# TensorE held back until the last table row has landed, then all four groups of four tiles in one go

## The chip, the core and the metric

The kernel runs on one core of one Trainium2 chip. The metric is the device time of one execution in microseconds (us), the median over runs. The core has a matrix engine (TensorE; PE in the rows), a vector engine (VectorE; DVE), an activation engine (ScalarE; ACT), GpSimd (POOL), which here only issues gathers, and SyncE (SP), which issues the plain transfers. Every engine works off its own list of instructions in order, and semaphores tie the lists together.

## What is computed

A batch of 2048 samples has 26 index fields and 13 dense values. Each index picks a row of 32 values from its field's table. From these rows the reference makes a linear term and a term over all products of pairs of fields, and a small network stands behind them:

```python
embed = tables[jnp.arange(FIELD_NUM)[None, :], sparse_inputs]      # 2048 x 26 x 32
p = jnp.einsum('bfe,bge->bfg', embed, embed)                       # 2048 x 26 x 26
l_z = jnp.einsum('bfe,feh->bh', embed, w_z)                        # h = 256
l_p = jnp.einsum('bfg,fgh->bh', p, w_p)
l_1 = relu(concatenate([l_z + l_p + l_b, dense_inputs], axis=-1))
h = relu(l_1 @ W1 + b1)                                            # 128
return sigmoid(h @ Wf + bf)
```

All of it is in float32.

## The kernel before

The batch is cut into 16 tiles of 128 samples, one sample per partition (`TILES`). Four tiles form a group, which the code calls a round (`ROUNDS` = 4, `TOGETHER` = 4), since one PSUM bank holds 4 x 128 columns. Each tile's 26 fields fall into two field groups (`GROUPS`): g = 0 has 16 fields in four transposes, g = 1 has 10 fields in three.

**The gather.** GpSimd issues one indirect transfer per tile and field, 16 x 26 = 416 in all (L221), tile after tile. Semaphore `landed[t][g]` counts the ones of tile t and field group g.

**The pair products.** For each tile ScalarE copies the rows of a field group into PSUM (`copy_fields`, L310, tile `ps_copy`) once they have landed; VectorE multiplies fields with fields (L252, `prod`) and adds up the products over the 32 values (L259, `pairs`). After the last rows of a tile have landed, one copy, four products and five sums are left, those of field group 1.

**The rounds on TensorE.** For each tile `turn(t)` transposes the gathered rows into PSUM `ps_turn` (L416; one bank for each field group), and the result is copied into `field_rows` (`lay`, L172 and L173). `turn_pairs(t)` transposes the pair sums into `ps_pair` (L433; three transposes), and they are copied into `pair_rows` (`lay_pairs`, L177). Once four tiles are there, `sum_lz(r)` runs 14 matmuls of 512 columns (L447) and `sum_lp(r)` six more (L458), both into `ps_h`. ScalarE makes the first hidden layer (`make_hidden0`, L333), TensorE multiplies it (`sum_h1`, L467 and L471), ScalarE makes the second (`make_hidden1`, L338), TensorE makes the logit (`sum_logit`, L476), ScalarE the sigmoid (`make_scores`, L344). The hidden layers of a round are interleaved with the transposes of the next one. A float32 matmul of 512 columns appears as two records in the trace.

**Who copies out of PSUM, and when.** `LATE` = 12. For tiles 0 to 11 ScalarE makes all the copies into `field_rows` and `pair_rows`; for tiles 12 to 15 it makes those of field group 0 and VectorE makes the rest, after all its pair products. ScalarE's list is written out by hand: between the `copy_fields` of tiles 0 to 15 stand the copies of tiles 0 to 7 and the hidden layers of round 0. So round 0's `sum_lz`, its `sum_lp` and the whole of round 1 up to its last `sum_lp` are fed while the gather runs; rounds 2 and 3 follow it. TensorE's own list has no wait of this kind: it goes on as soon as a tile has landed and the copies have freed the PSUM banks.

Of the kernel before, what the change touches and what calls it, by code (L numbers as in the profile page):

```python
# [26 lines left out]
def pnn_kernel(nc, dense, sparse, tables, w_z, w_low, w_high, l_b, W1, b1, Wf, bf, out):  # L27
# [21 lines left out]

    LATE = 12  # L50
# [25 lines left out]
    with ExitStack() as ctx:  # L76
# [69 lines left out]
        pairs_laid_act = sem("pairs_laid_act")  # L146
        pairs_laid_dve = sem("pairs_laid_dve")
# [11 lines left out]

        def laid_by_act(t):  # L160
            return NG * t if t <= LATE else NG * LATE + (t - LATE)

        def laid_by_dve(t):
            return max(0, t - LATE)

# [61 lines left out]
        def _(dve):  # L227
# [62 lines left out]
            for t in range(LATE, TILES):  # L290
                dve.wait_ge(turned, NG * t + 2)
                dve.wait_ge(lz_summed, t // TOGETHER)
                lay(nc.vector.tensor_copy, t, 1).then_inc(laid_dve, 1)
                if t > LATE:
                    dve.wait_ge(pairs_turned, t)
                    dve.wait_ge(h0_summed, (t - 1) // TOGETHER)
                    lay_pairs(nc.vector.tensor_copy, t - 1).then_inc(pairs_laid_dve, 1)
            dve.wait_ge(pairs_turned, TILES)
            lay_pairs(nc.vector.tensor_copy, TILES - 1).then_inc(pairs_laid_dve, 1)

        @block.scalar
        def _(act):
# [16 lines left out]

            def lay_pair_rows(t):  # L320
                if t >= TOGETHER:
                    act.wait_ge(h0_summed, t // TOGETHER)
                act.wait_ge(pairs_turned, t + 1)
                lay_pairs(nc.scalar.copy, t).then_inc(pairs_laid_act, 1)
# [22 lines left out]

            BOTH = range(NG)
            for t in range(TILES):
                copy_fields(t)  # L350
                if t < 4:
                    lay_rows(t, BOTH)
                    if t:
                        lay_pair_rows(t - 1)
                elif t == 7:
                    lay_pair_rows(3)
                elif t == 8:
                    make_hidden0(0)
                elif t == 9:
                    lay_rows(4, BOTH)  # L360
                    make_hidden1(0)
                elif t == 10:
                    lay_rows(5, BOTH)
                    make_scores(0)
                    lay_pair_rows(4)
                elif t == 11:
                    lay_rows(6, BOTH)
                    lay_pair_rows(5)
                elif t == 12:
                    lay_rows(7, BOTH)  # L370
                    lay_pair_rows(6)
            lay_pair_rows(7)
            for r in range(2, ROUNDS):
                make_hidden0(r - 1)
                for k in range(TOGETHER):
                    t = TOGETHER * r + k
                    lay_rows(t, BOTH if t < LATE else [0])
                    if k == 0:
                        make_hidden1(r - 1)
                    if k == 1:  # L380
                        make_scores(r - 1)
                    if k and t <= LATE:
                        lay_pair_rows(t - 1)
                if TOGETHER * (r + 1) <= LATE:
                    lay_pair_rows(TOGETHER * (r + 1) - 1)
# [5 lines left out]
        def _(pe):  # L391
# [44 lines left out]
            def sum_lz(r):  # L436
# [5 lines left out]
                if laid_by_dve(TOGETHER * (r + 1)):  # L442
                    pe.wait_ge(laid_dve, laid_by_dve(TOGETHER * (r + 1)))
# [84 lines left out]
```

## Time and profile before

| | us |
|---|---|
| median of 3 runs | 654.4 |
| lowest and highest of them | 652.64 and 654.55 |
| the profiled execution, whole | 653.79 |
| span of the profiled execution, first to last instruction | 652.0 |
| granted TensorE clock, mean share of full speed over the span | 0.688 |

Times in the rows are in us from the start of the span, durations as marked. In a row of the timeline the first number is the start and the second the duration of a merged run of instructions, "xN" their number, and the bracket the engine's idle time before it and what ended it. The clock column PEclk is the share of 2.4 GHz that TensorE was granted: 0.50 is 1.2 GHz, 1.00 is 2.4 GHz. The ends of matmuls are modelled, so their results can be ready later than the row says.

### The profile page before, as it was taken

Reading aid. Unit: us, or ns where it says so; the run is one execution under the profiler, and the core shown is the slowest. Engines: PE = TensorE matmul, PEld = TensorE weight load, DVE = VectorE, ACT = ScalarE, POOL = GpSimd, SP = SyncE. Lnnn points to the kernel's source line nnn. Section 1 sums busy time; section 2 is a strip of 40 time slices with the busy share of each in tenths; the row PEclk is TensorE's granted clock in tenths of the full one; section 3 lists DMA queues with packets and bytes.
Section 4 is the critical chain, followed back from the end, with each engine's and each line's share of the span. In section 5 each row is a group of like instructions: output and inputs, shape, how many; then the busy total and the mean of one; then the engine's idle time right before and its main releaser. Section 6 shows DMA issues by size and latency. Waiting matters only on the chain.

```text
span 652.0 us, 1736 instructions
## 1 busy us (share of the span) xinstructions
PE 136.6 (21%) x356; PEld 61.9 (9%) x356; DVE 436.1 (67%) x249; ACT 49.6 (8%) x102; POOL 417.8 (64%) x423
## 2 busy tenths in 40 slices
PE   0000000064000000310302010101800000449996
PEld 0000000031000000100001010100300000214442
DVE  3378787878787877666958767676859677650010
ACT  0000101010000000001001020101000000013201
POOL 6777777777777777677777777777777777200000
PEclk9999999997555555565556555555855555669997
DMA  6212121211121211111111112121111111000000
GB/s 138 13 14 13 13 14 13 13 13 13 13 13 13 13 12 12 12 12 12 11 12 12 12 12 12 11 13 12 11 13 11 11 12 13 5 0 1 0 1 1
DMA packets 18200, 9.06 MB, mean 14 GB/s; under 512 B 9536, under 2 KB 18189, under 8 KB 18189
## 3 DMA queue, kind: packets, MB, share of 16 engines
q0 software_dynamic: 13312, 6.84, 15.6%
q1 hardware_dynamic: 4878, 2.11, 1.3%
q14 instruction: 7, 0.06, 0.0%
q8 instruction: 3, 0.05, 0.0%
HBM read 8.91 MB, written 0.01 MB: 14 GB/s over the span
## 4 chain that ended last, share of the span: by engine, by line
POOL 58%; issue 27%; PE 8%; another core or an unknown queue 3%; ACT 2%; DMA 1%; DVE 0%; ACTq 0%
POOL rows L221 58%; PE ps_h L447 4%; PE ps_h L458 2%; PE ps_h L476 1%; PE ps_h L471 1%; ACT hidden L333 1%; PE ps_turn L416 1%; DMA rows<-in_L_rec_tables,which 1%; ACT field_rows L173 0%; PE ps_h L467 0%; PE ps_pair L433 0%; ACT scores L344 0%; DMA raw<-in_r_sparse_inputs 0%; ACT ps_copy L310 0%
## 5 line engine op out<-in xcount | busy, mean ns | idle before, releaser
L221 POOL DMA_INDIRECT rows<-in_L_rec_tables,which x416 | 417.0, 1002 | 141.0 <-issue 139.1
L252 DVE TENSOR_TENSOR prod<-ps_copy,rows 128x1536 f32<-128x1536 f32 (+6 forms) x128 | 219.4, 1745 | 138.9 <-issue 116.3
L259 DVE TENSOR_REDUCE pairs<-prod 128x96 f32<-128x3072 f32 (+2 forms) x96 | 216.6, 2270 | 0.0
L458 PE MATMUL ps_h<-pair_rows,w_pair 128*128 128x512 f32 x48 | 25.5, 688 | 209.8 <-issue 208.6
L416 PE MATMUL ps_turn<-ident,rows 128*128 128x128 f32 (+1 forms) x112 | 22.7, 351 | 221.2 <-DMA rows<-in_L_rec_tables,which 120.1
L447 PE MATMUL ps_h<-field_rows,wz 128*128 128x512 f32 (+1 forms) x112 | 55.0, 649 | 35.3 <-issue 34.2
L310 ACT COPY ps_copy<-rows 128x512 f32<-128x512 f32 (+1 forms) x32 | 16.3, 509 | 528.7 <-DMA rows<-in_L_rec_tables,which 528.7
L416 PEld LDWEIGHTS ps_turn<-ident,rows 128*128 128x128 f32 (+1 forms) x112 | 15.9, 173 | 231.0 <-issue 210.6
L458 PEld LDWEIGHTS ps_h<-pair_rows,w_pair 128*128 128x128 f32 x48 | 10.4, 225 | 222.6 <-issue 220.9
L447 PEld LDWEIGHTS ps_h<-field_rows,wz 128*128 128x128 f32 (+1 forms) x112 | 22.6, 208 | 65.7 <-issue 65.7
L172 DVE COPY field_rows<-ps_turn 64x128 f32<-64x128 f32 x4 | 1.1, 283 | 37.4 <-PE ps_turn L416 37.4
L173 ACT COPY field_rows<-ps_turn 128x512 f32<-128x512 f32 (+1 forms) x28 | 13.7, 488 | 10.0 <-remote 9.2
L467 PE MATMUL ps_h<-dense_T,w_dense 13*128 13x512 f32 x8 | 6.4, 884 | 34.8 <-issue 29.7
L471 PE MATMUL ps_h<-hidden,w 128*128 128x512 f32 x16 | 12.4, 917 | 0.0
L177 DVE COPY pair_rows<-ps_pair 128x384 f32<-128x384 f32 x4 | 2.2, 548 | 13.5 <-PE ps_pair L433 13.5
L433 PE MATMUL ps_pair<-ident,pairs 128*128 128x128 f32 x48 | 10.4, 335 | 3.4 <-issue 3.3
L433 PEld LDWEIGHTS ps_pair<-ident,pairs 128*128 128x128 f32 x48 | 6.7, 172 | 11.6 <-issue 10.8
L333 ACT ACTIVATE hidden<-ps_h,lb_col 128x512 f32<-128x512 f32 x8 | 5.1, 683 | 34.6 <-PE ps_h L458 25.1
L177 ACT COPY pair_rows<-ps_pair 128x384 f32<-128x384 f32 x12 | 5.8, 481 | 13.1 <-PE ps_pair L433 12.8
L476 PE MATMUL ps_h<-hidden,wf 128*1 128x512 f32 x8 | 6.3, 890 | 0.8 <-ACT hidden L338 0.8
L467 PEld LDWEIGHTS ps_h<-dense_T,w_dense 13*128 13x128 f32 x8 | 1.6, 244 | 36.4 <-issue 29.9
L271 DVE TENSOR_SCALAR dense_T<-ps_turn 13x512 f32<-13x512 f32 x4 | 2.7, 685 | 3.2 <-PE ps_turn L395 3.1
(23 smaller groups left out, 25.0 us busy)
## 6 DMA issues: line engine op xcount, KB each, us to landing
rows<-in_L_rec_tables,which POOLq DMA_INDIRECT x416
wz<-in_L_rec_w_z SPq DMA_DIRECT2D x1, 768.0 KB
w_pair<-in_w_low SPq DMA_DIRECT2D x1, 384.0 KB
w_back<-in_w_high SPq DMA_DIRECT2D x1, 384.0 KB
raw<-in_r_sparse_inputs SPq DMA_DIRECT2D x1, 182.0 KB, 2.4
w<-in_L_rec_W SPq DMA_DIRECT2D x1, 128.0 KB
dense_in<-in_r_dense_inputs SPq DMA_DIRECT2D x1, 104.0 KB, 3.2
wz<-in_L_rec_w_z SPq DMA_DIRECT2D x1, 64.0 KB
```

What stands on the lines that cost most here:

```text
L173: return copy(field_rows[:, first:whole, k, :], ps_turn[:, g, 0:(whole - first) * P].rearrange("p (j b) -> p j b", b=P))
L221: nc.gpsimd.indirect_dma_start(rows[:, t, E * f:E * (f + 1)], None, table_rows, bass.IndirectOffsetOnAxis(ap=which[:, t, f:f + 1], axis=0) ...
L252: ins = nc.vector.tensor_tensor(made.rearrange("p (g f) e -> p g f e", f=f1), own.broadcast_to([P, f1 - f0, f1, E]), others.broadcast_to([ ...
L259: nc.vector.tensor_reduce(pairs[:, t, first:end], prod[:, (NS * t + s) % PRODS, 0:end - first, :], AX.X, ALU.add).then_inc(summed, 1)
L310: nc.scalar.copy(ps_copy[:, g, 0:E * (end - first)], rows[:, t, E * first:E * end])\
L333: ins = nc.scalar.activation(hidden0[:, h, :], ps_h0[:, h, :], ACT.Relu, bias=lb_col[:, h:h + 1])
L416: ins = nc.tensor.transpose(ps_turn[0:n, g, (j - first) * P:(j - first + 1) * P], rows[:, t, j * P:j * P + n], ident[:, :])
L433: ins = nc.tensor.transpose(ps_pair[:, c * P:(c + 1) * P], pairs[:, t, c * P:(c + 1) * P], ident[:, :])
L447: ins = nc.tensor.matmul(ps_h0[:, h, :], wz[0:n, j, h * P:(h + 1) * P], field_rows[0:n, j, :, :].rearrange("p t b -> p (t b)"), start=(j = ...
L458: ins = nc.tensor.matmul(ps_h0[:, h, :], w_pair[:, c, h * P:(h + 1) * P], pair_rows[:, c, :, :].rearrange("p t b -> p (t b)"), start=False ...
L471: ins = nc.tensor.matmul(ps_h1[:, :], w1[:, h, :], hidden0[:, h, :], start=False, stop=(h == HALVES - 1))
L476: nc.tensor.matmul(logit, wf[:, :], hidden1[:, :], start=True, stop=True).then_inc(logit_made, 1)
```

## The change

`LATE` is gone, and with it the two semaphores for the pair copies, which become one (`pairs_laid`). Three things change.

First, TensorE waits, after the transposes of the dense inputs, for both field groups of tile 15 to have landed. Second, the copies are split for all tiles as they were for the last four: ScalarE lays field group 0, VectorE lays field group 1 and the pair sums. Third, ScalarE's list has all `copy_fields` first and then four rounds, and VectorE's list has all pair products first and then the copies of four rounds. GpSimd's and SyncE's lists and all matmuls stay as they are.

```diff
+            def move_pairs(t):
+                dve.wait_ge(pairs_turned, t + 1)
+                if t >= TOGETHER:
+                    dve.wait_ge(h0_summed, t // TOGETHER)
+                lay_pairs(nc.vector.tensor_copy, t).then_inc(pairs_laid, 1)
+
+            for r in range(ROUNDS):
+                for k in range(TOGETHER):
+                    t = TOGETHER * r + k
+                    dve.wait_ge(turned, NG * t + 2)
+                    if r:
+                        dve.wait_ge(lz_summed, r)
+                    lay(nc.vector.tensor_copy, t, 1).then_inc(laid_dve, 1)
+                    if k:
+                        move_pairs(t - 1)
+                move_pairs(TOGETHER * (r + 1) - 1)
...
             for t in range(TILES):
                 copy_fields(t)
-                if t < 4:
-                    lay_rows(t, BOTH)
-                    if t:
-                        lay_pair_rows(t - 1)
-                elif t == 7:
-                    lay_pair_rows(3)
-                elif t == 8:
-                    make_hidden0(0)
...
+            for r in range(ROUNDS):
+                if r:
+                    make_hidden0(r - 1)
                 for k in range(TOGETHER):
-                    t = TOGETHER * r + k
-                    lay_rows(t, BOTH if t < LATE else [0])
-                    if k == 0:
+                    lay_rows(TOGETHER * r + k, [0])
+                    if r and k == 0:
                         make_hidden1(r - 1)
-                    if k == 1:
+                    if r and k == 1:
                         make_scores(r - 1)
...
             pe.wait_ge(dense_made, 1)
 
+            for g in range(NG):
+                first, end = group_fields(g)
+                pe.wait_ge(landed[TILES - 1][g], DMA * (end - first))
+
             def turn(t):
...
                     if t:
-                        if t - 1 < LATE:
-                            pe.wait_ge(laid_act, laid_by_act(t - 1) + g + 1)
-                        elif g == 0:
-                            pe.wait_ge(laid_act, laid_by_act(t))
-                        else:
-                            pe.wait_ge(laid_dve, laid_by_dve(t))
+                        pe.wait_ge(laid_act if g == 0 else laid_dve, t)
```

On TensorE the order of the instructions is the same; the waits differ. Its list up to tile 1 was:

```order
L395 MATMUL ps_turn<-ident,dense_in 128x128 x3
L416 MATMUL ps_turn<-ident,rows 128x128 [waits landed_0_0,dense_made]
L416 MATMUL ps_turn<-ident,rows 128x128 x3
L416 MATMUL ps_turn<-ident,rows 128x128 [waits landed_0_1]
L416 MATMUL ps_turn<-ident,rows 128x128
L416 MATMUL ps_turn<-ident,rows 64x128
L416 MATMUL ps_turn<-ident,rows 128x128 [waits landed_1_0,laid_act]
L416 MATMUL ps_turn<-ident,rows 128x128 x3
L416 MATMUL ps_turn<-ident,rows 128x128 [waits landed_1_1,laid_act]
```

In the changed kernel the same place reads:

```order
L358 MATMUL ps_turn<-ident,dense_in 128x128 x3
L378 MATMUL ps_turn<-ident,rows 128x128 [waits landed_15_1,landed_0_0,landed_15_0,dense_made]
L378 MATMUL ps_turn<-ident,rows 128x128 x3
L378 MATMUL ps_turn<-ident,rows 128x128 [waits landed_0_1]
L378 MATMUL ps_turn<-ident,rows 128x128
L378 MATMUL ps_turn<-ident,rows 64x128
L378 MATMUL ps_turn<-ident,rows 128x128 [waits landed_1_0,laid_act]
L378 MATMUL ps_turn<-ident,rows 128x128 x3
L378 MATMUL ps_turn<-ident,rows 128x128 [waits landed_1_1,laid_dve]
```

The first transpose of tile 0 now waits for tile 15's rows, and the three transposes of tile 1's field group 1 now wait for VectorE instead of ScalarE.

On VectorE the end of the list, after the last pair sums of tile 15, was (rows of tile 12 first, then tiles 13 to 15):

```order
L259 TENSOR_REDUCE pairs<-prod 128x52 [waits multiplied]
L172 COPY field_rows<-ps_turn 64x128 [waits lz_summed,turned]
L173 COPY field_rows<-ps_turn 128x2x128
L172 COPY field_rows<-ps_turn 64x128 [waits lz_summed,turned]
L173 COPY field_rows<-ps_turn 128x2x128
L177 COPY pair_rows<-ps_pair 128x3x128 [waits h0_summed,pairs_turned]
```

In the changed kernel it goes on at the same place with tile 0:

```order
L250 TENSOR_REDUCE pairs<-prod 128x52 [waits multiplied]
L163 COPY field_rows<-ps_turn 64x128 [waits turned]
L164 COPY field_rows<-ps_turn 128x2x128
L163 COPY field_rows<-ps_turn 64x128 [waits turned]
L164 COPY field_rows<-ps_turn 128x2x128
L168 COPY pair_rows<-ps_pair 128x3x128 [waits pairs_turned]
```

The first copy that VectorE makes for TensorE was tile 12's and is now tile 0's; both stand behind the last pair sum of tile 15.

On ScalarE the list behind the last `copy_fields` was, from tile 15 on, with the copies of tile 8 after the hidden layer:

```order
L310 COPY ps_copy<-rows 128x320 [waits landed_15_1,multiplied]
L177 COPY pair_rows<-ps_pair 128x3x128 [waits pairs_turned,h0_summed]
L333 ACTIVATE hidden<-ps_h,lb_col 128x512 [waits h0_summed,h1_summed]
L333 ACTIVATE hidden<-ps_h,lb_col 128x512
L173 COPY field_rows<-ps_turn 128x4x128 [waits turned,lz_summed]
L172 COPY field_rows<-ps_turn 64x128 [waits turned]
L173 COPY field_rows<-ps_turn 128x2x128
L338 ACTIVATE hidden<-ps_h,b_col 128x512 [waits h1_summed]
```

Now it is:

```order
L307 COPY ps_copy<-rows 128x320 [waits landed_15_1,multiplied]
L164 COPY field_rows<-ps_turn 128x4x128 [waits turned] x4
L324 ACTIVATE hidden<-ps_h,lb_col 128x512 [waits h0_summed,mlp_in]
L324 ACTIVATE hidden<-ps_h,lb_col 128x512
L164 COPY field_rows<-ps_turn 128x4x128 [waits turned,lz_summed]
L329 ACTIVATE hidden<-ps_h,b_col 128x512 [waits h1_summed]
L164 COPY field_rows<-ps_turn 128x4x128 [waits turned,lz_summed]
L335 ACT_TABLE_LOAD
L335 ACTIVATE scores<-ps_h,bf_one 1x4x128 [waits logit_made]
```

The four copies of tiles 0 to 3, the hidden layers of round 0 and the load of the sigmoid's table have moved from the time of the gather to behind it.

## Rows read from the trace of the kernel before

**Rows 1.** The page: busy us of each engine, share of the span, instructions.

```profile
PE 136.6 (21%) x356; PEld 61.9 (9%) x356; DVE 436.1 (67%) x249; ACT 49.6 (8%) x102; POOL 417.8 (64%) x423
```

**Rows 2.** Timeline, GpSimd: the first issue, a slow one, the last.

```profile
3.51 1.10 POOL L221 DMA_INDIRECT rows<-in_L_rec_tables,which  x1 [1.92 <-DVE which L238]
...
259.51 1.94 POOL L221 DMA_INDIRECT rows<-in_L_rec_tables,which  x1 [0.61 <-issue]
...
558.67 0.94 POOL L221 DMA_INDIRECT rows<-in_L_rec_tables,which  x1 [0.30 <-issue]
```

**Rows 3.** Stretches: length, then busy time of each engine (instructions), clock, DMA share, GB/s.

```profile
224.00:271.00 47.00, 0.00 (x0) 0.00 (x0) 33.97 (x18) 1.83 (x4) 35.41 (x36) 0.50 0.17 12
500.00:560.00 60.00, 0.00 (x0) 0.00 (x0) 42.85 (x23) 1.61 (x3) 45.14 (x43) 0.50 0.18 12
```

**Rows 4.** Timeline from the last landing to the end of the pair sums.

```profile
562.02 0.43 ACT L310 COPY ps_copy<-rows 128x320 f32<-128x320 f32 x1 [13.52 <-DMA rows<-in_L_rec_tables,which]
...
576.60 3.53 DVE L259 TENSOR_REDUCE pairs<-prod 128x48 f32<-128x1536 f32 x2
```

**Rows 5.** Timeline: round 1's last matmuls, tile 8's transposes, ScalarE waiting for them.

```profile
562.91 6.95 PE L458 MATMUL ps_h<-pair_rows,w_pair 128*128 128x512 f32 x12 [92.70 <-issue]
...
569.70 0.93 PE L416 MATMUL ps_turn<-ident,rows 128*128 128x128 f32 x7
...
572.32 1.27 ACT L333 ACTIVATE hidden<-ps_h,lb_col 128x512 f32<-128x512 f32 x2 [9.46 <-remote]
...
582.82 0.59 ACT L173 COPY field_rows<-ps_turn 128x512 f32<-128x512 f32 x1 [9.23 <-remote]
...
586.27 0.26 ACT L172 COPY field_rows<-ps_turn 64x128 f32<-64x128 f32 x1 [2.86 <-remote]
...
586.85 0.90 PE L416 MATMUL ps_turn<-ident,rows 128*128 128x128 f32 x3 [2.27 <-ACT field_rows L173]
```

**Rows 6.** Timeline, tile 0 during the gather: transposes, then ScalarE's copies.

```profile
38.88 0.90 PE L416 MATMUL ps_turn<-ident,rows 128*128 128x128 f32 x3 [11.31 <-DMA rows<-in_L_rec_tables,which]
...
39.32 2.06 DVE L252 TENSOR_TENSOR prod<-ps_copy,rows 128x1824 f32<-128x1824 f32 x1 [3.38 <-issue]
39.82 0.26 ACT L172 COPY field_rows<-ps_turn 64x128 f32<-64x128 f32 x1
```

**Rows 7.** Timeline, the end of round 2 and the whole of round 3.

```profile
607.00 5.42 PE L458 MATMUL ps_h<-pair_rows,w_pair 128*128 128x512 f32 x12 [0.62 <-ACT pair_rows L177]
...
613.22 0.28 DVE L172 COPY field_rows<-ps_turn 64x128 f32<-64x128 f32 x1 [33.09 <-PE ps_turn L416]
613.43 0.41 DVE L173 COPY field_rows<-ps_turn 128x256 f32<-128x256 f32 x1
...
616.71 0.93 PE L416 MATMUL ps_turn<-ident,rows 128*128 128x128 f32 x7
...
617.65 1.02 PE L476 MATMUL ps_h<-hidden,wf 128*1 128x512 f32 x2
...
622.10 12.45 PE L447 MATMUL ps_h<-field_rows,wz 128*128 128x512 f32 x28 [0.47 <-DVE field_rows L173]
...
635.67 5.42 PE L458 MATMUL ps_h<-pair_rows,w_pair 128*128 128x512 f32 x12 [0.65 <-DVE pair_rows L177]
```

**Rows 8.** Timeline, in the gather: `sum_lz` twice, seven transposes, the sigmoid's table.

```profile
138.16 14.74 PE L447 MATMUL ps_h<-field_rows,wz 128*128 128x512 f32 x28
...
344.73 1.75 PE L416 MATMUL ps_turn<-ident,rows 128*128 128x128 f32 x7 [29.61 <-issue]
...
381.46 1.28 ACT L344 ACT_TABLE_LOAD   x1
...
454.39 15.35 PE L447 MATMUL ps_h<-field_rows,wz 128*128 128x512 f32 x28 [34.24 <-issue]
```

**Rows 9.** Stretches after the gather, same columns as Rows 3.

```profile
590.00:593.00 3.00, 2.79 (x22) 2.05 (x20) 0.00 (x0) 2.99 (x9) 0.00 (x0) 1.00 0.00 0
...
600.00:641.00 41.00, 38.60 (x117) 17.35 (x115) 4.50 (x12) 5.53 (x9) 0.00 (x0) 1.00 0.00 0
```

More of the change, by code:

```diff
@@ L48, in pnn_kernel @@
     PRODS = 3
-    LATE = 12
     def pairs_before(c):
@@ L145, in pnn_kernel @@
         pairs_turned = sem("pairs_turned")
-        pairs_laid_act = sem("pairs_laid_act")
-        pairs_laid_dve = sem("pairs_laid_dve")
+        pairs_laid = sem("pairs_laid")
         h0_summed = sem("h0_summed")
@@ L288, in _ @@
                         add_up(t, s - 1)
[L290 to L299, printed above, removed]
+            def move_pairs(t):
[13 more added lines that the diff above has]
+                move_pairs(TOGETHER * (r + 1) - 1)
         @block.scalar
@@ L318, in lay_rows @@
                     lay(nc.scalar.copy, t, g).then_inc(laid_act, 1)
[L320 to L324, printed above, removed]
             def make_hidden0(r):
@@ L345, in make_scores @@
                     .then_inc(scored, 1)
-            BOTH = range(NG)
             for t in range(TILES):
                 copy_fields(t)
-                if t < 4:
-                    lay_rows(t, BOTH)
-                    if t:
-                        lay_pair_rows(t - 1)
-                elif t == 7:
-                    lay_pair_rows(3)
-                elif t == 8:
-                    make_hidden0(0)
[L359 to L374, printed above, removed]
+            for r in range(ROUNDS):
+                if r:
+                    make_hidden0(r - 1)
                 for k in range(TOGETHER):
-                    t = TOGETHER * r + k
-                    lay_rows(t, BOTH if t < LATE else [0])
-                    if k == 0:
+                    lay_rows(TOGETHER * r + k, [0])
+                    if r and k == 0:
                         make_hidden1(r - 1)
-                    if k == 1:
+                    if r and k == 1:
                         make_scores(r - 1)
[L382 to L385, printed above, removed]
             make_hidden0(ROUNDS - 1)
@@ L420, in pairs_moved @@
             def pairs_moved(t):
-                if t < LATE:
-                    pe.wait_ge(pairs_laid_act, t + 1)
-                else:
-                    pe.wait_ge(pairs_laid_dve, t + 1 - LATE)
+                pe.wait_ge(pairs_laid, t + 1)
             def turn_pairs(t):
@@ L440, in sum_lz @@
                     pe.wait_ge(scored, r)
-                pe.wait_ge(laid_act, laid_by_act(TOGETHER * (r + 1)))
-                if laid_by_dve(TOGETHER * (r + 1)):
-                    pe.wait_ge(laid_dve, laid_by_dve(TOGETHER * (r + 1)))
+                pe.wait_ge(laid_act, TOGETHER * (r + 1))
+                pe.wait_ge(laid_dve, TOGETHER * (r + 1))
                 for j in range(CH):
```

4 lines of the change are left out of this document (removed).

## The prediction

> **What bounds the kernel now.** I read the busy shares first, then GpSimd's timeline, then everything behind the last landing. No engine is full: VectorE has 67% and GpSimd 64%, TensorE only 21% [rows 1]. The reader is to see two phases. The first is the gather. GpSimd starts its first issue at 3.51 and its last at 558.67 [rows 2], 415 steps of 1.338 us on the mean. A regular step, as the last row shows it, is 0.94 or 0.95 busy and 0.30 idle, 1.25 us; a slow issue takes up to 1.94 us [rows 2]. VectorE is paced by this: 436.1 us for 16 tiles [rows 1] are 27.3 us a tile, against 26 x 1.338 = 34.8 us in which a tile's rows arrive. The second phase is what is left when the last rows have landed, seen at ScalarE's copy at 562.02 and VectorE's last pair sums, which start at 576.60 and take 3.53, to 580.13 [rows 4]. From there to the end of the span at 652.0 are 71.87 us, and they hold mostly rounds 2 and 3 of TensorE and the last hidden layers. Rounds 0 and 1 up to their last `sum_lp` were laid out over the gather.
>
> **What the wait itself costs.** TensorE's new wait ends at about 562.0, when tile 15's rows are there. It then transposes tile 0 and field group 0 of tile 1 and stops: field group 1 of tile 1 needs the bank that VectorE must copy out, and in VectorE's list that copy stands behind the last pair sum. So the restart is set by VectorE at 580.13, not by the landing at 562.02 [rows 4]. TensorE's wait hides under VectorE's work and costs nothing by itself; what costs is that all four rounds now come behind 580.13. Queued behind TensorE's wait is all of its list; nobody in the gather waits for any of it, since `copy_fields` and the pair products need only landings and each other. VectorE's 24 copies into `field_rows` and 12 into `pair_rows` that are new in its list all stand behind 580.13 too.
>
> **Term a, from 580.13 to the first `sum_lz`.** VectorE lays tile 0's second field group: 0.21 from the first copy to the second and 0.41 for that, 0.62 us [rows 7]. Behind this TensorE has 17 transposes of rows (three of tile 1, seven each of tiles 2 and 3) and nine of pair sums, 26 in all, and each copy of VectorE or ScalarE fits under the transposes that follow. Seven took 1.75 at the slow clock, 0.25 each [rows 8], and 0.93 at the full one, 0.133 each [rows 7]. So the 26 take 3.5 to 6.5 us; TensorE has been idle and starts at 1.2 GHz, and the last one's own latency is in a row of seven but once, so I take 5.5, or 6.1 with the 0.62. Bounds of the term: 4.1 and 7.1.
>
> **Term b, `sum_lz` of round 0.** At full clock it is 12.45 [rows 7]; in the gather, begun after idling, it took 14.74 and 15.35 [rows 8], so 2.9 us more at half speed means that the clock rose 5.8 us after the start. Round 1's `sum_lp` at 562.91 took 6.95 against 5.42 [rows 5, 7], a rise after 3.1 us. If the transposes of term a count as activity, the clock rises 3.1 to 5.8 us after 580.8, at or just after the start of `sum_lz`. That they may is seen before 590: TensorE transposes at 586.85, has one logit behind that, and the granted clock is 1.00 from 590 [rows 5, 9]. I take 12.7; the bounds are 12.45 and 15.35.
> The Trainium skill, page "TensorE: Matmul & The Clock Gate", section "Part 4: PE-mode transpose", says that the full clock does not engage for transposes. By that rule term b is one of the 14.74 to 15.35 of the gather; the stretch at 590 speaks against it, though a logit stands among its transposes. It is weighed among the rivals.
>
> **Term c, the rest of round 0.** From the end of `sum_lz` at 634.55 to the end of `sum_lp` at 641.09 in round 3, with the pair transposes and VectorE's copy between: 6.54 us [rows 7]. So round 0 ends at 580.13 + 6.1 + 12.7 + 6.54 = 605.5.
>
> **Term d, rounds 1 to 3.** Each is built as round 3 is now: the same split of the copies, the hidden layers of the round before among the transposes. From the end of `sum_lp` at 612.42 to the next at 641.09 are 28.67 us [rows 7], with the clock at 1.00 throughout [rows 9]. Three times 28.67 = 86.0.
>
> **Term e, the sigmoid's table.** ScalarE loaded it in the gather, 1.28 us [rows 8]. Now the load stands in round 1, between the copy of tile 5 and the sigmoid. It starts under the logit (1.02 us, [rows 7]), and tile 6's copy comes late by what is left: 0.65 us as I lay it against round 3. Bounds 0.3 and 1.28.
>
> **Term f, the tail.** The last hidden layers, the sigmoid and the store, unchanged: 652.0 - 641.09 = 10.91 us.
>
> **The sum.** 605.5 + 86.0 + 0.65 + 10.91 = 703.0 of span. The profiled execution is 1.79 longer than its span (653.79 against 652.0) and the median is 0.61 above it, so 705.4 us for the median, 51 us or 7.8% slower. As a cross-check against before: two rounds more behind 580.13 are 57.3, the table 0.65, and the first round there takes 25.3 (580.13 to 605.5) instead of 32.3 (580.13 to round 2's end at 612.42), 7 less. That gain is because ScalarE waited after 562 for results that TensorE's rows show as long finished: its copies at 582.82 and 586.27 stand behind transposes that ran at 569.70 [rows 5].
>
> **Rivals.**
> A cold start. The transposes of term a don't raise the clock, and round 0's `sum_lz` takes 14.74 or 15.35 as in the gather [rows 8]: 2.0 to 2.7 more, 707.4 to 708.1. For it: in the gather transposes stood ahead of it too, and it began slow. Against it: there they were seven and three, not 26. 0.12. (The Trainium skill's page on the clock gate would have this one.)
> Late results at the restart. What happened to tile 8's transposes could happen to those that TensorE does at 562: VectorE's first copy would start when ScalarE's did then, 586.27, not 580.13. That is 6.1 more: 711.5. For it speaks that in both cases VectorE is in the same products; against it that tile 0's transposes at 38.88, beside the same kind of product, were copied at 39.82 at once [rows 6], and that in the case of rows 5 matmuls of 512 columns ran just before. 0.06.
> The gather gets quicker because TensorE is quiet. With 1.25 us at every step, the last issue comes at 3.51 + 415 x 1.25 = 522.3, 36.4 us earlier, and VectorE, at 27.3 us a tile, still keeps up: 669.0. Against it: TensorE is idle from 224 to 271 and from 500 to 560, and GpSimd makes only 36 and 43 issues there, 1.31 and 1.40 us a step [rows 3], with a slow one of 1.94 at 259.51 [rows 2]. 0.05.
> The Trainium skill, page "DMA: Bandwidth & Descriptors", section "SWDGE vs HWDGE vs iDMA", says that GpSimd writes its descriptors into SBUF state that VectorE can lock it out of. By that the slow steps are VectorE's doing and stay, which gives 705.4; if they were TensorE's, it would be the 669.0 above.
> The clock stays low in the rounds. At 1.2 GHz a round's 12.45 + 5.42 us and some 4 of hidden layers nearly double, about 20 more in each of four: 785. Against it the 1.00 of the whole stretch from 600 to 641 [rows 9]. 0.02.
> The other side. TensorE's quiet would have to free GpSimd of its idle gaps as well: at 0.95 us a step the gather would end far ahead of VectorE, whose 436.1 us [rows 1] would then set the end of the pair sums: 16 issues of 1.25 and a landing put its start near 26, its end near 462, 118 us earlier than 580: 587. It decides from a step of 1.338 - 51/415 = 1.215 us, and no stretch that I looked at, idle TensorE or not, is below 1.25 [rows 2, 3]. 0.01.
> That the change doesn't do what it says, TensorE going past tile 1 before 580, is excluded by VectorE's order, and would be worth the 6.1 of term a at most.
>
> **How the numbers follow.** Forecast, 705.4, chance 0.74; the rivals 0.12, 0.06, 0.05, 0.02 and 0.01. The range goes from 699 to 713 and leaves out only the last three. Its low end takes the lower bound of term a (2.0), the distance of the lowest of the three runs before from their median (1.8) and 2.5 us of drift in the gather; a stretch such as 500 to 560 would give back 60 - 43 x 1.25 = 6.2 [rows 3]. Its high end is the late results, 711.5, with part of a cold start. The noise of a measurement is about 0.3%, 2 us; every case but the last rival is slower by far more. So faster 0.01, same 0.01 for what lies between, slower 0.98.
>
> **What would show it.** Right: TensorE's rows empty from 8 to 562; tile 1's second field group transposed at about 580.8; the first `sum_lz` at about 586 and 12.5 to 13 long; ends of `sum_lp` 28.7 apart, the last near 692; clock 1.00 between. Wrong: a last landing far from 562 (the gather depends on TensorE after all), a gap between 580 and the restart (late results), a `sum_lz` of 15 in round 0 or more in later ones (the clock), or rounds longer than 28.7, where a hand-over between VectorE and TensorE would have become the bound.

## The result, and the profile after

The changed kernel takes 707.37 us, the median of four runs (706.79 to 707.99), against 653.52 for the kernel before beside it (652.37 to 654.55). The ratio is 1.0825, with a 95% interval of 1.0799 to 1.085. The forecast was 705.4, slower, in a range of 699 to 713. The time came out as forecast. One term of the sum did not, and the runs showed that its cause reaches much further than the 3.8 us that it cost here.

The page of the changed kernel, busy time of each engine and then the busy tenths of TensorE and the granted clock in 40 slices of the span of 705.9; they answer [rows 1].

```profile
PE 114.7 (16%) x356; PEld 54.6 (8%) x356; DVE 449.6 (64%) x285; ACT 39.4 (6%) x66; POOL 418.3 (59%) x423
...
PE   0000000000000000000000000000000118899996
...
PEclk9999999999999999999999999999999999999998
```

TensorE's work has gone from 136.6 to 114.7 us because nearly all of its matmuls now run at the full clock, and all of it but the dense inputs' transposes stands behind 561. It is the same 356 records in less engine time, and 54 us more in all: the busy share says nothing of what a kernel costs. The clock row is to be read with care. It shows 9 from the start, with TensorE idle, and up to 586 it stands at 1.00 while seven transposes take 1.70 us, as long as at half the clock (1.75, [rows 8]). So up to there the pace of the records tells the clock, and the row does not. From 588 to 589.18 it reads 0.50, and from 590 on 1.00, as the records do.

The stretches [rows 3] in the changed kernel (length, busy time of PE, PEld, DVE, ACT and POOL with instructions, clock, DMA share, GB/s), and the rounds:

```profile
224.00:271.00 47.00, 0.00 (x0) 0.00 (x0) 33.82 (x18) 1.45 (x3) 35.56 (x35) 1.00 0.17 12
500.00:560.00 60.00, 0.00 (x0) 0.00 (x0) 42.01 (x23) 1.61 (x3) 44.21 (x42) 1.00 0.18 12
600.00:700.00 100.00, 91.76 (x290) 42.24 (x289) 14.06 (x37) 17.68 (x27) 0.00 (x0) 1.00 0.00 0
```

GpSimd makes 35 and 42 issues where it made 36 and 43: the gather is what it was. Its last issue starts at 557.81, 0.86 earlier than [rows 2].

The timeline from the last landing to the first `sum_lz` of the changed kernel (start, duration, engine, line; in brackets the idle time before and what ended it) answers [rows 4, 5]:

```profile
561.18 0.43 ACT L307 COPY ps_copy<-rows 128x320 f32<-128x320 f32 x1 [13.69 <-DMA rows<-in_L_rec_tables,which]
561.34 2.88 PE L378 MATMUL ps_turn<-ident,rows 128*128 128x128 f32 x11 [552.31 <-DMA rows<-in_L_rec_tables,which]
...
569.16 0.59 ACT L164 COPY field_rows<-ps_turn 128x512 f32<-128x512 f32 x1 [6.10 <-remote]
...
575.76 3.53 DVE L250 TENSOR_REDUCE pairs<-prod 128x48 f32<-128x1536 f32 x2
579.21 0.27 DVE L163 COPY field_rows<-ps_turn 64x128 f32<-64x128 f32 x1
...
580.56 0.85 PE L392 MATMUL ps_pair<-ident,pairs 128*128 128x128 f32 x3
...
581.20 1.70 PE L378 MATMUL ps_turn<-ident,rows 128*128 128x128 f32 x7
...
585.25 0.56 DVE L168 COPY pair_rows<-ps_pair 128x384 f32<-128x384 f32 x1 [3.83 <-remote]
...
585.99 0.59 ACT L164 COPY field_rows<-ps_turn 128x512 f32<-128x512 f32 x1 [16.25 <-remote]
...
589.18 12.78 PE L405 MATMUL ps_h<-field_rows,wz 128*128 128x512 f32 x28 [0.16 <-DVE field_rows L164]
```

The restart is where the prediction put it, behind VectorE's pair sums. But VectorE's third hand-over, the copy of tile 0's pair sums, waits 3.83 us for transposes that TensorE's row has finished at 581.41, and ScalarE's copy of tile 2 waits until 585.99. Only from 586 on do results come at once.

TensorE's rows of the changed kernel, round 0's `sum_lp` and the last one:

```profile
603.19 5.39 PE L416 MATMUL ps_h<-pair_rows,w_pair 128*128 128x512 f32 x12 [0.74 <-DVE pair_rows L168]
...
632.56 5.42 PE L416 MATMUL ps_h<-pair_rows,w_pair 128*128 128x512 f32 x12 [0.65 <-DVE pair_rows L168]
...
661.23 5.42 PE L416 MATMUL ps_h<-pair_rows,w_pair 128*128 128x512 f32 x12 [0.65 <-DVE pair_rows L168]
...
689.90 5.42 PE L416 MATMUL ps_h<-pair_rows,w_pair 128*128 128x512 f32 x12 [0.65 <-DVE pair_rows L168]
```

The ends are 608.58, 637.98, 666.65 and 695.32: 29.40, 28.67 and 28.67 apart. The first distance holds the 0.7 us that the load of the sigmoid's table adds.

### The profile page after: what moved, and what is told of

Same layout as the page of the kernel before. It is cut to its first block, busy times and chain, and to the rows that moved or that the text cites. A ratio compares the mean times of both kernels' runs of the same rounds, so it can differ in the third digit from the quotient of the medians.

```text
span 705.9 us, 1746 instructions
## 1 busy us (share of the span) xinstructions
PE 114.7 (16%) x356; PEld 54.6 (8%) x356; DVE 449.6 (64%) x285; ACT 39.4 (6%) x66; POOL 418.3 (59%) x423
## 4 chain that ended last, share of the span: by engine, by line
issue 74%; PE 14%; ACT 4%; POOL 3%; another core or an unknown queue 3%; DVE 1%; DMA 1%; ACTq 0%
PE ps_h L405 7%; POOL rows L212 3%; PE ps_h L416 3%; ACT ps_copy L307 2%; PE ps_h L429 1%; PE ps_turn L378 1%; ACT hidden L324 1%; PE ps_h L425 1%; PE ps_h L434 1%; PE ps_pair L392 1%; ACT field_rows L164 0%; DMA rows<-in_L_rec_tables,which 0%; DVE pair_rows L168 0%; DMA raw<-in_r_sparse_inputs 0%
## 5 line engine op out<-in xcount | busy, mean ns | idle before, releaser
L378 PE MATMUL ps_turn<-ident,rows 128*128 128x128 f32 (+1 forms) x112 | 18.5, 313 | 568.8 <-DMA rows<-in_L_rec_tables,which 552.3
L405 PE MATMUL ps_h<-field_rows,wz 128*128 128x512 f32 (+1 forms) x112 | 50.1, 601 | 1.6 <-DVE field_rows L164 1.6
L168 DVE COPY pair_rows<-ps_pair 128x384 f32<-128x384 f32 x16 | 8.8, 550 | 57.4 <-PE ps_pair L392 53.5
L163 DVE COPY field_rows<-ps_turn 64x128 f32<-64x128 f32 x16 | 4.5, 282 | 35.2 <-PE ps_turn L378 35.0
L416 PE MATMUL ps_h<-pair_rows,w_pair 128*128 128x512 f32 x48 | 21.6, 600 | 2.7 <-DVE pair_rows L168 2.7
L164 ACT COPY field_rows<-ps_turn 128x512 f32<-128x512 f32 x16 | 9.4, 586 | 26.8 <-remote 22.3
L429 PE MATMUL ps_h<-hidden,w 128*128 128x512 f32 x16 | 8.5, 656 | 0.0
L164 DVE COPY field_rows<-ps_turn 128x256 f32<-128x256 f32 x16 | 6.5, 406 | 0.0
L425 PE MATMUL ps_h<-dense_T,w_dense 13*128 13x512 f32 x8 | 4.5, 636 | 3.5 <-ACT hidden L324 3.5
L335 ACT ACTIVATE scores<-ps_h,bf_one 1x512 f32<-1x512 f32 x4 | 4.5, 1117 | 3.2 <-PE ps_h L434 3.2
```

The costliest lines, as they stand in the source:

```text
L164: return copy(field_rows[:, first:whole, k, :], ps_turn[:, g, 0:(whole - first) * P].rearrange("p (j b) -> p j b", b=P))
L378: ins = nc.tensor.transpose(ps_turn[0:n, g, (j - first) * P:(j - first + 1) * P], rows[:, t, j * P:j * P + n], ident[:, :])
L405: ins = nc.tensor.matmul(ps_h0[:, h, :], wz[0:n, j, h * P:(h + 1) * P], field_rows[0:n, j, :, :].rearrange("p t b -> p (t b)"), start=(j = ...
L416: ins = nc.tensor.matmul(ps_h0[:, h, :], w_pair[:, c, h * P:(h + 1) * P], pair_rows[:, c, :, :].rearrange("p t b -> p (t b)"), start=False ...
L429: ins = nc.tensor.matmul(ps_h1[:, :], w1[:, h, :], hidden0[:, h, :], start=False, stop=(h == HALVES - 1))
```

## The experiments

The experiments fell on four chips of two kinds, which the time of the kernel before tells apart. On two it takes 653 us, the first kind; by its time the pair of the result is of it. On the other two it takes 604 us, the second kind. Each chip was used for one group of runs only, so whether a chip stays of its kind isn't shown; "kind" names what was measured. Each experiment says its kind. A kernel is compared only with the kernel before on its own chip. "The theory" is that of the prediction: the restart waits for VectorE's list.

### The wait taken away

From the changed kernel:

```diff
-            for g in range(NG):
-                first, end = group_fields(g)
-                pe.wait_ge(landed[TILES - 1][g], DMA * (end - first))
```

> The changed kernel without TensorE's wait for tile 15's rows; the lists of ScalarE and VectorE stay as changed. My theory: the wait costs nothing, since TensorE stops at tile 1's second field group until VectorE is through with its pair sums at about 579; 707 us as with it, within 0.3%. Rival: the wait itself, or TensorE's early work, moves the end by more than 2 us.

708.43 us (706.41 to 709.71), ratio 1.0835 [1.0802, 1.0868] to 653.11 beside it, first kind. The wait costs nothing: with it or without it TensorE stands still until VectorE's and ScalarE's lists let it go on. The change's title names the wait, and its price comes from the order of the two other lists.

Something else is to be seen in the profiled execution, of 709.46 us. Round 0's `sum_lz` takes 14.86 us, against 12.78 in the changed kernel. These are its first four records:

```profile
588.58 3.75 PE L401 MATMUL ps_h<-field_rows,wz 128*128 128x512 f32 x4 [0.16 <-DVE field_rows L164]
```

They take 0.94 us each where a record at full clock takes 12.45 / 28 = 0.44, and the granted clock reads 0.50 from 588.5 to 593. That is the size of the prediction's cold start.

### The wait alone

To the kernel before, whose lists stay as they were, the same three lines are added ahead of the transposes.

> The kernel before with TensorE's new wait alone, lists of ScalarE and VectorE as before. ScalarE then waits at tile 0's copy for TensorE, so the products of tiles 1 to 15 come behind the gather: 563 + 15 x 27.3 = 973, and rounds 2 and 3 and the tail behind it: about 1045 us.

This ran on a chip of the second kind: 973.57 us, one execution, beside 604.28. ScalarE and VectorE at the landing of the last rows:

```profile
526.87 3.52 PE L420 MATMUL ps_turn<-ident,rows 128*128 128x128 f32 x14 [518.65 <-DMA rows<-in_L_rec_tables,which]
528.00 0.59 ACT L173 COPY field_rows<-ps_turn 128x512 f32<-128x512 f32 x1 [488.74 <-PE ps_turn L420]
...
529.68 5.68 DVE L252 TENSOR_TENSOR prod<-ps_copy,rows 128x512 f32<-128x512 f32 x4 [472.74 <-ACT ps_copy L310]
```

In the old order ScalarE's copies of tile 0 stand ahead of its `copy_fields` of later tiles. Waiting for TensorE, it starves VectorE, which then does 15 of its 16 tiles behind the gather. Behind 529.68 these are 15 tiles of 26.4 us, to 925.9, and the end of round 2 and round 3 follow. The expectation was 71 us too high; 36 of that is the landing, which it took from the other kind. The wait is free only because the change also puts every `copy_fields` first.

### ScalarE makes all copies of round 0

For tiles 0 to 3 ScalarE also lays field group 1 and the pair sums, so that round 0 needs nothing of VectorE:

```diff
-                    lay_rows(TOGETHER * r + k, [0])
+                    lay_rows(TOGETHER * r + k, [0] if r else range(NG))
+                    if r == 0 and k:
+                        lay_pair_rows(k - 1)
```

> The changed kernel, but ScalarE makes all copies of tiles 0 to 3 (both field groups and pair sums), so TensorE's round 0 can run beside VectorE's last products. My theory (VectorE's list sets the restart): round 0 begins at 561 instead of 579 and ends 18 us earlier; 689 us, or 691 to 695 if results reach ScalarE late as at 569 in the changed kernel. Rival (the restart is set by something else, such as the landing or a cold TensorE): 707.

707.50 us (706.6 to 708.07), ratio 1.0827 [1.0802, 1.0852]: nothing gained, a miss by the theory. ScalarE after the landing, on a chip of the first kind:

```profile
563.61 0.59 ACT L167 COPY field_rows<-ps_turn 128x512 f32<-128x512 f32 x1 [0.86 <-PE ps_turn L395]
...
570.70 0.59 ACT L167 COPY field_rows<-ps_turn 128x512 f32<-128x512 f32 x1 [5.92 <-remote]
...
577.00 0.26 ACT L166 COPY field_rows<-ps_turn 64x128 f32<-64x128 f32 x1 [5.72 <-remote]
...
584.00 0.48 ACT L171 COPY pair_rows<-ps_pair 128x384 f32<-128x384 f32 x1 [6.47 <-remote]
...
586.81 0.59 ACT L167 COPY field_rows<-ps_turn 128x512 f32<-128x512 f32 x1 [2.33 <-remote]
```

VectorE's order is out of the path, and another wait takes its place that ends at the same time: each result of TensorE that ScalarE needs comes 6 to 7 us behind the last one, until 586. `sum_lz` starts at 589.91, against 589.18 in the changed kernel. So on this chip two things end together at the restart, and taking VectorE's order out of it brings nothing. VectorE's list alone would let `sum_lz` begin at 579.29 + 6.1 = 585.4, the late results alone at 589.9; that the two lie so close is chance.

The same kernel and the changed one were then run on a chip of the second kind.

> The changed kernel once more, on the chip of this group. The runs so far fell on two chips: on one the kernel before takes 653 us, GpSimd's steps slow down from 224 on and TensorE's results come late until about 586; on the other it takes 604, every step is 1.25 us and results are prompt. On the first kind of chip: 707. On the second: the pair sums end at 544.8, and the terms of my prediction stand behind it, 6.1 + 12.7 + 6.5 + 86.0 + 0.65 + 10.9 and 1.8 around the span: 669 to 670.

> The changed kernel with ScalarE making all copies of tiles 0 to 3, which gained nothing on the chip with late results (707.5). If the late results swallowed the gain there and VectorE's list sets the restart where they are prompt: 18 us under the changed kernel on a chip of the second kind, 651 to 652; equal to it on one of the first kind. Rival: the restart is set by something else on both, and it is equal on both.

The changed kernel takes 666.39 us there (666.01 to 668.42), ratio 1.1048 [1.1021, 1.1074] to 603.84. With ScalarE's copies it takes 649.61 (649.2 to 650.67), 16.8 less, where 18 were expected. Here the theory holds. The changed kernel on that chip:

```profile
539.93 3.54 DVE L250 TENSOR_REDUCE pairs<-prod 128x48 f32<-128x1536 f32 x2
543.38 0.27 DVE L163 COPY field_rows<-ps_turn 64x128 f32<-64x128 f32 x1
...
545.61 0.56 DVE L168 COPY pair_rows<-ps_pair 128x384 f32<-128x384 f32 x1
...
549.53 12.45 PE L405 MATMUL ps_h<-field_rows,wz 128*128 128x512 f32 x28 [0.47 <-DVE field_rows L164]
```

VectorE's copy of the pair sums, which waited 3.83 us above, starts without a wait, and from the end of the pair sums at 543.47 to `sum_lz` are 6.06 us. The forecast of this term was 6.1.

With ScalarE's copies, on the same chip, TensorE's transposes of tile 3:

```profile
531.26 0.94 PE L395 MATMUL ps_turn<-ident,rows 128*128 128x128 f32 x7
```

The seven of tile 2, at 529.12, took 1.70. So the pace nearly doubled when TensorE had made nothing but transposes since the start of the kernel. Round 0's `sum_lz` follows at 533.06 and takes 12.45.

### VectorE's products taken away

All products and pair sums are left out; the pair sums are zero, so the pair part of the result is not computed. ScalarE's and TensorE's waits for them go too. The rest of the changed kernel stays.

```diff
-            nc.vector.memset(pairs[:, :, NPAIRS:NP], 0.0).then_inc(pairs_zeroed, 1)
+            nc.vector.memset(pairs[:, :, :], 0.0).then_inc(pairs_zeroed, 1)
...
-                        multiply(t, s)
...
-                        add_up(t, s - 1)
```

> The changed kernel without the pair products and sums on VectorE (the pair sums are zero); gather, copies and rounds stay. Two theories of the late results and of GpSimd's slow steps. If VectorE's products cause them: GpSimd's last issue comes at about 523 instead of 558, and from the landing to the end all results are prompt: 650 us. If they come with the gather itself: last issue still at about 558, restart at 561, results late by 3 to 10 us in all until about 585: 689 us.

707.87 us, one execution, first kind: as slow as with the products, which neither theory expected. The two stretches of the gather, and what followed the landing:

```profile
224.00:271.00 47.00, 0.00 (x0) 0.00 (x0) 0.00 (x0) 1.45 (x3) 35.26 (x35) 1.00 0.18 12
500.00:560.00 60.00, 0.00 (x0) 0.00 (x0) 0.00 (x0) 1.65 (x4) 43.38 (x42) 1.00 0.18 12
```

```profile
560.13 3.52 PE L366 MATMUL ps_turn<-ident,rows 128*128 128x128 f32 x14 [551.67 <-DMA rows<-in_L_rec_tables,which]
...
561.89 0.28 DVE L163 COPY field_rows<-ps_turn 64x128 f32<-64x128 f32 x1 [546.36 <-PE ps_turn L366]
...
567.96 0.59 ACT L164 COPY field_rows<-ps_turn 128x512 f32<-128x512 f32 x1 [6.13 <-remote]
...
574.26 0.28 DVE L163 COPY field_rows<-ps_turn 64x128 f32<-64x128 f32 x1 [11.76 <-remote]
...
581.96 0.56 DVE L168 COPY pair_rows<-ps_pair 128x384 f32<-128x384 f32 x1 [7.09 <-remote]
```

Two things follow. VectorE and TensorE are both still in the stretches, and GpSimd makes its 35 and 42 issues all the same: the slow steps are neither's doing. The rule of the Trainium skill that the prediction weighed (page "DMA: Bandwidth & Descriptors", section "SWDGE vs HWDGE vs iDMA") lets VectorE lock GpSimd out in a two-port mode of VectorE; by this run it doesn't explain the slow steps of this kernel, since they come with VectorE idle. And TensorE's late results don't come from VectorE's work either. They come as a pace: tile 0's seven transposes are there at once, at 561.89, the next four 6.1 us later, then three after 6.3, then three after 7.7, which is 1.5, 2.1 and 2.6 us a record.

### Plain loads in place of the gather

The 416 indirect transfers are replaced by 32 plain ones, which bring other rows of the tables; all else of the changed kernel is the same work on these rows.

```diff
+                    sp.dma_start(rows[:, t, E * first:E * end], part[:, E * first:E * end]).then_inc(landed[t][g], DMA)
...
-                    nc.gpsimd.indirect_dma_start(
```

> The changed kernel with the gather left out: 32 plain transfers bring other rows of the tables, so values differ, and all compute stays. VectorE is then the bound: 16 x 27.3 = 436 us of products from about 12 on, 450, and 127 behind it: 577 us if results are late at the restart as now. If lateness comes with the gather, results at the restart are prompt, no wait over 1 us there, and it is 573.

562.41 us, one execution, on the same chip of the first kind. VectorE now never waits for rows, and its pair sums end at 433.96 + 3.53 = 437.49. What follows:

```profile
433.96 3.53 DVE L247 TENSOR_REDUCE pairs<-prod 128x48 f32<-128x1536 f32 x2
...
439.65 0.56 DVE L168 COPY pair_rows<-ps_pair 128x384 f32<-128x384 f32 x1
...
443.98 12.45 PE L402 MATMUL ps_h<-field_rows,wz 128*128 128x512 f32 x28 [0.47 <-DVE field_rows L164]
```

6.5 us from the pair sums to `sum_lz` and no late result. So the lateness on this chip comes with the gather; the plain transfers are long through when TensorE restarts, so whether other transfers beside it would do the same isn't shown. The sum was expected too high because a tile of VectorE took 26.4 us without the gaps of waiting, not 27.3. The prediction's terms behind the pair sums, 6.1 + 12.7 + 6.54 + 86.0 + 0.65 + 10.91 = 122.9, meet 560.6 - 437.49 = 123.1.

### An earlier pair copy

In the kernel before ScalarE lays tile 3's pair sums behind `copy_fields(7)`, although TensorE's row shows them transposed by 155. Here it does so behind `copy_fields(4)`.

```diff
-                elif t == 7:
+                elif t == 4:
                     lay_pair_rows(3)
```

> The kernel before with one copy of ScalarE moved: tile 3's pair sums are copied after tile 4's fields (at about 169) instead of after tile 7's (270). TensorE's rows show these transposes at 154.8. If its results really come late after a sum_lz in the gather, ScalarE waits until about 215 and the fields of tile 5 (188.9 before) are copied only then; the end hardly moves, 654, since VectorE has 7 us of slack a tile. If they are prompt, the copy stands at 169.4 without a wait.

605.25 us, one execution, against 604.28: no difference. It ran on a chip of the second kind, where the copy found its result at once:

```profile
169.24 0.47 ACT L177 COPY pair_rows<-ps_pair 128x384 f32<-128x384 f32 x1
...
541.24 3.54 DVE L259 TENSOR_REDUCE pairs<-prod 128x48 f32<-128x1536 f32 x2
...
545.24 12.45 PE L447 MATMUL ps_h<-field_rows,wz 128*128 128x512 f32 x28 [0.56 <-ACT field_rows L173]
```

For the first kind, where the question arose, it decides nothing. But its last two rows price the lateness in the kernel before. Here round 2's `sum_lz` starts 0.5 us behind the end of the pair sums (544.78); on the first kind it starts at 593.45, 13.3 us behind 580.13.

### More of the rounds in the gather

If holding TensorE back costs, letting it go further should pay. First ScalarE's list of the kernel before was moved up, so that round 1 and most of round 2 fall into the gather:

```diff
-            lay_pair_rows(7)
-            for r in range(2, ROUNDS):
+                elif t == 12:
+                    lay_pair_rows(7)
+                elif t == 13:
+                    make_hidden0(1)
+                    lay_rows(8, BOTH)
...
+            for r in range(3, ROUNDS):
```

> The kernel before with ScalarE's copies moved the other way: rounds 1 and 2 are pulled into the gather, so that behind the last landing only round 2's last pair sums and sum_lp and round 3 are left. If what counts is how much of TensorE's rounds stands behind the pair sums: 654 less about 22 = 632 us. Rival: results of TensorE come late in the gather (tens of us behind a sum_lz), ScalarE waits for them, its copies for VectorE come late and the pair sums end later: 654 or more.

> The kernel before with round 1 and most of round 2 pulled into the gather. On a chip of the second kind 584 against 604, as measured. On one of the first kind the late results (some 50 us behind a sum_lz, if the semaphore's times can be believed) may make ScalarE wait and its copies for VectorE late: 635 if they don't, 654 or more if they do.

583.91 us (583.08 to 584.91), ratio 0.9656 [0.9638, 0.9674], and 581.33 (580.28 to 583.15), ratio 0.9629 [0.9601, 0.9658], both on chips of the second kind: 20.4 and 22.5 us less than the kernel before, as the 22 expected.

Then ScalarE laid every tile right behind its `copy_fields`, with `LATE` = 16 and no copy left for VectorE:

```diff
+                r, k = divmod(t, TOGETHER)
+                if r and k == 0:
+                    lay_pair_rows(t - 1)
+                    make_hidden0(r - 1)
+                lay_rows(t, BOTH)
...
+                if k:
+                    lay_pair_rows(t - 1)
+            lay_pair_rows(TILES - 1)
```

> The kernel before with no round held back: ScalarE lays each tile behind its fields, so rounds 0 to 2 finish in the gather and round 3's sum_lz runs beside VectorE's last products. Behind the last landing stay VectorE's 18 us, one pair copy, sum_lp and the hidden layers: on a chip of the second kind 544.8 + 0.9 + 0.6 + 5.4 + 10.9 + 1.8 = 564 us. On one of the first kind: 600 if results are late only where nobody waits, 654 or more if ScalarE waits for them in the gather and VectorE falls behind.

564.51 us (563.74 to 565.54), ratio 0.9351 [0.933, 0.9371], on a chip of the second kind: 39 us less than the kernel before, as expected. On that kind it is the fastest version here.

> The version that lays each tile as it lands, measured once more. If the kernel before takes about 604 us beside it, this repeats 564 us, 40 us less. If the kernel before takes about 654, the gather ends near 562 and VectorE's pair sums near 580; then two theories part. If TensorE's results come late until about 586 as they did beside the kernel before and the changed one, tile 15's copies wait and the first sum_lz of round 3 cannot begin before about 589: 589 + 12.5 + 6.5 + 10.9 of rest gives a span near 619 and a time near 621 us. If the results are prompt, or the late ones reach only the last pair sums, sum_lz ends near 577 to 583 and the time is 600 to 606 us.

744.78 us (744.72 to 745.58) against 653.33, ratio 1.1392 [1.1342, 1.1442]. The same kernel that is 6.5% faster on one chip is 13.9% slower on another. Neither time of this expectation had it; the expectation of the run before had the mechanism, ScalarE waiting in the gather and VectorE falling behind, at 654 or more. The page's tenths of VectorE and GpSimd, and ScalarE's timeline, a copy behind round 0's `sum_lz` and then round 1:

```profile
DVE  3486888879000006788996000000396999999990
...
POOL 6777777777777777777777777777770000000000
```

```profile
214.22 0.48 ACT L177 COPY pair_rows<-ps_pair 128x384 f32<-128x384 f32 x1 [45.27 <-issue]
...
374.57 0.48 ACT L177 COPY pair_rows<-ps_pair 128x384 f32<-128x384 f32 x1 [7.93 <-remote]
374.95 0.95 ACT L308 COPY ps_copy<-rows 128x512 f32<-128x512 f32 x2
460.67 0.48 ACT L177 COPY pair_rows<-ps_pair 128x384 f32<-128x384 f32 x1 [84.77 <-issue]
494.28 1.27 ACT L331 ACTIVATE hidden<-ps_h,lb_col 128x512 f32<-128x512 f32 x2 [33.13 <-remote]
505.47 0.59 ACT L173 COPY field_rows<-ps_turn 128x512 f32<-128x512 f32 x1 [9.93 <-remote]
513.82 0.26 ACT L172 COPY field_rows<-ps_turn 64x128 f32<-64x128 f32 x1 [7.76 <-remote]
```

The reader is to count TensorE's records between two results. From 374.57 to 460.67 they are the 28 of `sum_lz` and three pair transposes: 86.10 / 31 = 2.78 us each. To 494.28 they are the 12 of `sum_lp`: 33.61 / 12 = 2.80. To 505.47 four transposes: 2.80 each, and to 513.82 three: 2.78. A record of 512 columns and one of 128 cost the same, so the work in a record doesn't set the pace: something lets one record's result through every 2.8 us. Whether the matmuls themselves come late or only the news of their end, no row tells. TensorE's own rows hide it:

```profile
366.79 14.26 PE L422 MATMUL ps_h<-field_rows,wz 128*128 128x512 f32 x28 [18.78 <-issue]
380.98 0.55 PE L408 MATMUL ps_pair<-ident,pairs 128*128 128x128 f32 x3
461.20 7.79 PE L433 MATMUL ps_h<-pair_rows,w_pair 128*128 128x512 f32 x12 [79.68 <-issue]
```

They show 14 us of matmul and 80 of idling. ScalarE works its list in order, so its next `copy_fields` stands behind the copy that waits, VectorE gets nothing to multiply, and its idle time ahead of products is 284.3 us in all, against 103.0 on the second kind. Behind 586 results are prompt again, but VectorE still has five tiles of 26.4 us ahead of it at 591.69. In the kernel before, on this kind of chip, results are seen late only behind 562 [rows 5]. That the same pace runs under its gather is likely, not shown: there each copy of TensorE's results stands long behind its transposes and starts without a wait.

## Why the prediction was right

The sum, term by term, in us; the last column is the changed kernel on the chip of the second kind.

| | predicted | measured | other kind |
|---|---|---|---|
| end of the pair sums | 580.13 | 579.29 | 543.47 |
| a, to the first `sum_lz` | 6.1 | 9.89 | 6.06 |
| b and c, to the end of round 0 | 19.24 | 19.40 | 19.06 |
| d and e, three rounds and the table | 86.65 | 86.74 | 86.73 |
| f, tail | 10.91 | 10.58 | 9.18 |
| span | 703.0 | 705.9 | 664.5 |

**The wait is free, the order costs.** Right, and shown from both sides: without the wait the time is the same, and the wait without the new order costs 369 us.

**What sets the restart.** VectorE's list, said the prediction. On the second kind that is shown: 16.8 us come back when round 0 is taken out of it. On the kind of the result it isn't: nothing came back, since the late results would have held `sum_lz` until 589 by themselves. That the restart still came near its forecast is in part luck.

**Term a** was mis-sized: 9.89 measured against 6.1, 3.8 us more and beyond its upper bound of 7.1. The step that failed is "the 26 take 3.5 to 6.5 us": it priced the transposes from rows of TensorE alone. On the chip with prompt results they take just that, 5.4. On this one their results came late until 586. The prediction had seen this in ScalarE's waits [rows 5] and made it a rival, but for the first copy only, and gave it 6.1 us. The first copies behind a rest were prompt and the later ones were not, so part of that rival came true inside the term. That the total still fell 2 us from the forecast is in part luck: the pair sums ended 0.84 us earlier and the tail was 0.33 shorter. It is luck too that the pair of the result ran on a chip of the kind from which the landing at 562 was read; on the other kind the changed kernel takes 666.39, far below the range.

**Term b, the clock.** The rival of a cold start, as it was put, fell: that transposes don't raise the clock. `sum_lz` of round 0 took 12.78, not 14.74, and 12.45 on the other kind. The rule of the Trainium skill (page "TensorE: Matmul & The Clock Gate", section "Part 4: PE-mode transpose") isn't borne out: with ScalarE's copies on the second kind seven transposes sped up from 1.70 to 0.94 us before any other matmul had run. But the price of the rival did come on the first kind, where late results spread the transposes: `sum_lz` took 14.86 without the wait, 14.12 without the products and 13.53 with ScalarE's copies, against 12.45 in the three executions with prompt results (plain loads, and the two on the second kind). So 12.7 was a good choice for prompt results, and 12.78 here was one draw from a spread of 2 us.

**Terms c to f** were read from a round of the same build [rows 7] and came within 0.4 us each in the changed kernel. The table's 0.65 is seen as a wait of 0.64 ahead of tile 7's transposes, which wait for the copy of tile 6. The tail of 9.18 in the last column is the clock and not the kind of chip: its last two groups of matmuls took 1.98 and 1.02 us there, and 2.54 and 1.86 in the changed kernel of the result, which is the whole 1.4; the version with the earlier pair copy has 1.86 on the second kind too.

**The gather.** It did not get quicker with TensorE still, nor with VectorE still. Its slow steps come with the kind of chip: on the second kind the last issue starts at 521.99, and a step is 1.25 us throughout.

**The cross-check's gain of 7** was 3.0: the first round behind the pair sums took 29.29 us where that of the kernel before took 32.29. It stood for the late results that the kernel before meets ahead of round 2, and the changed kernel met some of its own. Where results are prompt there is no such gain, and the change costs 62.6 us instead of 53.9.

## What to carry to other kernels

Price a restart, and every hand-over, by the time at which the consumer gets the result, not by the end of the producer's row. When a wait is added, ask what the new order of the other engines' lists costs; the wait itself may be free. In a list that is worked in order, a copy that waits for another engine should stand well behind what it waits for, and a version that lets them follow closely should be measured on more than one chip before it is called faster.

## What the hardware showed

- **Two kinds of chip.** The same kernel before took 652 to 656 us on some chips and 603 to 605 on others. 35 us of the difference are the gather: from about 224 us on, the first kind makes 35 or 36 issues in 47 us where the second makes 38. The other 13 are the late results ahead of round 2.
- **A pace of 2.8 us for each matmul record** on the first kind, while a gather runs, whatever the record's size. It was measured in the version that lays each tile as it lands. Behind the last issue results still come late, at 1.5 to 2.6 us a record, and until about 586, 27 to 30 us behind that issue. It was absent on the same kind with plain loads, and on the second kind with the gather. Behind a rest of TensorE the first records are prompt (seven at 561.89 in the kernel without products) and the following ones slow down, as if a supply had filled while it rested; that is a picture, not a finding. What is supplied, or what holds it up, no row shows, and no run was made that could tell. Whether the slow steps of GpSimd and this pace have one cause is open; they don't begin together. In the version above `sum_lz`, begun at 137.74, and three transposes are in ScalarE's hands only at 214.22, while GpSimd's steps are regular from 17 until 231.
- **The clock and transposes.** Behind a rest of 517 us TensorE made only transposes and went to the full pace within them (1.70, then 0.94 us for seven, second kind). Where late results spread its transposes, the next `sum_lz` began slow and took up to 14.86 us instead of 12.45.
- **What stays open of the kernel itself:** no version here is shown to beat the kernel before on the first kind. The one with part of round 2 pulled in was measured on the second kind alone.
